# Flamingo block with a two-of-eight expert layer: the order of gathers, indexed stores and weight parts on GpSimd, and products of ones on TensorE

## The reference

```
logits = xf @ Wr + br
topk_val, topk_idx = top_k(logits, 2);  scores = softmax(topk_val)
h = xf @ W1[e] + b1[e];  a, g = split(h);  out_e = (silu(a) * g) @ W2[e] + b2[e]
out = sum over the two chosen e of scores * out_e
```

## Time and profile before

| what | value |
|---|---|
| median of 3 runs | 936.27 us (932.23, 936.27, 938.24) |
| the profiled execution's own time | 931.24 us |
| its span, first to last instruction | 929.4 us |
| mean granted TensorE clock | 0.985 of full speed |
| TensorE busy / VectorE / ScalarE / GpSimd | 95% / 60% / 56% / 40% |
| DMA queues of SyncE and of GpSimd, share of 16 engines | 21.3% and 3.4% |

### The profile page before, as it was taken

The page is one execution under the profiler, slowest core; times in us unless marked ns, Lnnn a source line. Parts: engine busy times, 40 slices in busy tenths (PEclk is TensorE's granted clock), DMA queues, the critical chain, the costliest instruction groups (busy, mean ns, idle before and its releaser), DMA issues.

```text
span 929.4 us, 20316 instructions
## 1 busy us (share of the span) xinstructions
PE 880.3 (95%) x6813; PEld 799.1 (86%) x6814; DVE 560.4 (60%) x1331; ACT 519.2 (56%) x1466; POOL 367.2 (40%) x530
## 2 busy tenths in 40 slices
PE   6989999999999979999999976999999999999996
PEld 4579999998898759999999976899999999987653
DVE  4666556556655763444434347877777876666456
ACT  6676777677776244344343452756655655652565
POOL 3173444444443224445454541434434443443000
PEclk9999999999999889999999998999999999999998
DMA  9000000420002457777776713000000000000002
GB/s 264 4 1 2 1 1 1 148 69 1 0 1 72 144 204 249 250 242 261 244 262 236 267 42 94 24 23 13 13 23 11 12 1 1 1 2 0 1 0 91
DMA packets 36674, 76.19 MB, mean 82 GB/s; under 512 B 4941, under 2 KB 22721, under 8 KB 36481
## 3 DMA queue, kind: packets, MB, share of 16 engines
q1 hardware_dynamic: 32865, 65.11, 21.3%
q0 software_dynamic: 3744, 10.23, 3.4%
HBM read 66.02 MB, written 9.31 MB: 81 GB/s over the span
## 4 chain that ended last, share of the span: by engine, by line
PE 85%; DVE 6%; DMA 3%; issue 2%; ACT 2%; POOL 1%; SPq 0%; DVEq 0%; POOLq 0%; ACTq 0%
PE banks L535 16%; PE banks L537 15%; PE banks L536 15%; PE banks L1530 14%; PE banks L573 8%; PE banks L563 5%; PE banks L427 2%; PE banks L1809 2%; PE banks L1820 1%; PE banks L1814 1%; PE banks L1802 1%; PE banks L1520 1%; PE banks L542 1%; DMA y_rows<-region_b,home_now 1%; DVE region_b L1404 1%
## 5 line engine op out<-in xcount | busy, mean ns | idle before, releaser
L1084 ACT ACTIVATE region_a<-banks,negmax 128x154 f32<-128x154 f32 (+1 forms) x384 | 161.7, 434 | 29.1 <-DVE negmax L877 28.0
L1530 PE MATMUL banks<-region_b,region_a 128*128 128x128 f32 x1248 | 148.4, 278 | 1.2 <-ACT region_b L1565 1.2
L1530 PEld LDWEIGHTS banks<-region_b,region_a 128*128 128x128 f32 x1248 | 145.4, 195 | 1.8 <-ACT region_b L1565 0.9
L1230 POOL TENSOR_TENSOR region_a<-region_a,recip 128x640 f32<-128x640 f32 x64 | 80.3, 1255 | 137.4 <-DVE recip L881 137.4
L1193 POOL TENSOR_TENSOR region_a<-region_a,recip 128x512 f32<-128x512 f32 x64 | 66.7, 1042 | 138.6 <-DVE recip L881 99.5
L877 DVE TENSOR_REDUCE negmax<-banks 128x4 f32<-128x616 f32 (+1 forms) x128 | 100.4, 785 | 28.3 <-PE banks L563 15.5
L1620 DVE SCALAR_TENSOR_TENSOR region_b<-banks,region_a,region_b 128x128 f32<-128x128 f32 x156 | 43.9, 344 | 104.3 <-PE banks L1530 104.3
L573 PE MATMUL banks<-ident,region_a 128*128 128x128 f32 x640 | 94.5, 279 | 3.9 <-DVE pT_low L887 1.6
L573 PEld LDWEIGHTS banks<-ident,region_a 128*128 128x128 f32 x640 | 72.7, 141 | 14.2 <-issue 9.8
L535 PE MATMUL banks<-xT_high,Wq_high 128*128 128x256 f32 x256 | 77.8, 304 | 3.8 <-DVE q_low L863 2.0
L1066 ACT CAST pT_high<-banks 128x640 fp32r<-128x640 f32 x64 | 44.4, 694 | 65.1 <-PE banks L573 65.1
(11 more groups left out here) (294 smaller groups left out, 2495.0 us busy)
## 6 DMA issues: line engine op xcount, KB each, us to landing
region_a<-in_L_ffn_W SPq DMA_DIRECT2D x39, 1024.0 KB, 5.4
W<-in_L_ffn_W SPq DMA_DIRECT2D x1, 4096.0 KB, 15.9
W<-y_rows SPq DMA_DIRECT2D x16, 256.0 KB, 2.8
out<-x SPq DMA_DIRECT2D x8, 256.0 KB, 2.2
x<-in_x SPq DMA_DIRECT2D x1, 1536.0 KB, 13.7
region_b<-in_L_xattn_Wq SPq DMA_DIRECT2D x1, 1024.0 KB, 9.4
region_b<-in_L_xattn_Wo SPq DMA_DIRECT2D x1, 1024.0 KB, 14.6
xn_rows<-region_b SPq DMA_DIRECT2D x1, 1024.0 KB, 4.8
```

Of the source, the lines that this page charges most:

```text
L1084: e = act.activation(into, source, ACT.Exp, bias=negmax[:, n % 2, u:u + 1], accum_out=sums[:, n % 2, u:u + 1])
L1230: pool.tensor_tensor(probs1[:, n % 2], probs1[:, n % 2], rc, ALU.mult).then_inc(sem("p_norm"), 1)
L1530: mm = pe.matmul(banks[:, 2 * r + part, m * P:(m + 1) * P], W1[r][:, k, cols], xgT[:, r, k, :], start=(k == 0), stop=(k == DK - 1))
```

## The change

Three edits.

1. GpSimd: in turn j the gather is that of slot j + 4 in place of slot j + 3, still ahead of the store of slot j. The gather of slot 3 moves ahead of turn 0. With it go the waits: `xgt_ps` and `token_now_ready` for j + 2, and the copy of row numbers is that of slot j + 5.
2. GpSimd: the four query weight parts move behind the store of their turn.
3. TensorE: 16 products of ones ahead of the first slot's transpose, and 12 in place of 16 behind the wait for `gathered0`.

```diff
@@ pe_pairs
                 pe.wait_ge(sem("gathered0"), 16)
-                pe_warm(pe, 16)
+                pe_warm(pe, 12)
             pe.wait_ge(sem("xn_ready"), t0 + 2)
@@ pe_experts
             pe.wait_ge(sem("kv1_raw"), len(KV1_UNITS) - 2)
+            pe_warm(pe, 16)
             turn_x(0, 0)
@@ pool_experts
             home_next(0, 0)
+            pool.wait_ge(sem("token_now_ready"), 1)
+            pool.wait_ge(sem("xgt_ps"), 1)
+            pool.wait_ge(sem("xg_in1"), 16)
+            tokens_now(RING + 1, 1)
+            gather_x(0)
 
             def emit(i):
                 for j, r in body_tiles(i):
-                    if is_tile(j + 3):
-                        pool.wait_ge(sem("token_now_ready"), j + 1)
-                        pool.wait_ge(sem("xgt_ps"), j + 1)
                     if is_tile(j + 4):
-                        ahead, more = after(r, 1)
+                        pool.wait_ge(sem("token_now_ready"), j + 2)
+                        pool.wait_ge(sem("xgt_ps"), j + 2)
+                    if is_tile(j + 5):
+                        ahead, more = after(r, 2)
                         pool.wait_ge(sem(f"xg_in{ahead}"), 16 * (i + more + 1))
-                        tokens_now(j + 4, ahead)
-                    if is_tile(j + 3):
-                        gather_x(r)
-                    if query_part(j) is not None:
-                        n = query_part(j)
-                        pool.wait_ge(sem("query_high"), n + 1)
-                        pool.tensor_tensor(Wq_low_parts[:, n], Wq1_parts[:, n], Wq_high_parts[:, n].bitcast(F32),
-                                           ALU.subtract).then_inc(sem("query_low"), 1)
+                        tokens_now(j + 5, ahead)
+                    if is_tile(j + 4):
+                        gather_x(after(r, 1)[0])
                     pool.wait_ge(sem("home_now_ready"), j + 1)
                     pool.wait_ge(sem("ey_sb"), j + 1)
...
                     scatter_y(r)
+                    if query_part(j) is not None:
+                        n = query_part(j)
+                        pool.wait_ge(sem("query_high"), n + 1)
+                        pool.tensor_tensor(Wq_low_parts[:, n], Wq1_parts[:, n], Wq_high_parts[:, n].bitcast(F32),
+                                           ALU.subtract).then_inc(sem("query_low"), 1)
```

## The result

The changed kernel took 928.65 us in the median (926.03 to 932.60, 20 runs), the kernel before 935.59 us (931.35 to 940.14, 20 runs) beside it. The ratio is 0.9924, 95% interval 0.9909 to 0.9939: 6.9 us less. The forecast was 4.7 us less; the time lies in its range and in the case "within 1%". The two intervals do not overlap. In five measurements the median of the kernel before was 932.2 to 936.2 us, that of the changed kernel 928.7 and 929.5 us in two. All ratios here are of fast runs with fast runs, and they are not the quotients of the two medians.

A forecast was written before the change was run, and what follows sets the result against it. TensorE was taken as the bound (85% of the span), its steady 5.22 us turn unchangeable. Gains of 2.8 + 1.8 + 0.1 + 0 = 4.7 us from the 936.27 us median gave 931.5 us, range 925.5 to 937.

The forecast's parts named there:

- within 1%: Whole kernel: the change cannot be told from no change, since a measurement resolves about 1%; chance 0.83.
- Part 1: 16 products of ones fill TensorE's idle gap ahead of slot 0, so its hidden products run at full clock; 2.8 us.
- this just fits, by 0.3 us: Opening: VectorE, after `b2` lands at 345.2 us, finishes at 347.7 us; TensorE needs it for slot 0's output at 348.0.
- Rival A: Opening is bound by loads: `b2` or W1 comes 3 us later and the ones gain nothing; 934.4 us, chance 0.12.
- rival B: Slot 0's low clock is not in every launch, so ones ahead of it may gain nothing; about 934.4 us, chance 0.13.
- Part 2: Gathers issued one slot sooner on GpSimd remove TensorE's stall at slot 37's late transpose; 1.8 us.
- in other turns gathers are already in time: Expert stage outside slot 37: more lead for the gathers buys nothing.
- rival C: More gathers are late in ordinary runs than in the profiled one, so more is gained; 926.6 us, chance 0.15.
- Part 3: Query parts behind GpSimd's stores: slot 36's store goes out sooner, easing slot 37's; 0.1 us, between 0 and 1.3.
- Part 4: 12 ones behind `gathered0` start attention 1's transposes 0.4 to 0.6 us sooner, but VectorE's weight part hides it; 0.
- The end of the stage: Expert stage's last two stores keep their distance from TensorE's last products, being tied to VectorE's addition and the previous landing.
- Rival D: Two gathers under way beside a store make stores land later, 5.7 us per turn; 949.6 us, chance 0.04.

The follow-up runs named there:

- the slow launch: Kernel before with 24 products of ones ahead of slot 0, profiled on its slowest run, 939.46 us; measured 0.9976, median 934.74 against 936.20 us.

## Why the prediction was right, and where it was too small

The direction, the case and the range were right, and the mechanisms that the sum named are in the trace. Its sizes were off both ways, so it is in part luck that the sum of 4.7 us lies between the two measured gains, 6.9 and 3.3 us.

- **Part 1, predicted 2.8 us.** The step "at full clock slot 0's hidden products take what slot 1's take" held where at most 1.01 us were idle behind the ones: 3.84 us in three of three profiles (idle 0.61, 0.45, 1.01 us). It failed in two of two with 1.83 and 1.86 us idle: 5.47 and 5.41 us. The step "nothing is delayed, the gap hides all of it" took the gap of before, 3.75 us, as given: it is 3.5 to 4.1 us without the ones and 4.0 to 5.4 us with 16 of them. And "this just fits, by 0.3 us" failed. The landing of `b2`, put at 345.2 us, was sound; the step from it to the multiply was put at nothing and measures 1.26 to 1.31 us in the twelve profiles where `b2` stands behind W1 and its landing was recorded, the one of before among them. With it the prediction's own numbers give 349.0 us against the 348.0 that TensorE needs. The trace lost 0.5 us and not 1.0, since slot 1's products themselves came 0.46 us later than predicted (9.86 us behind the key and value products, not 9.40). The term was 2.35 - 0.49 = 1.9 us in the changed kernel's profile.

  Over all profiles, slot 2's hidden products start 17.2 to 17.6 us behind the key and value products without the ones, 15.5 to 15.8 us with 16 of them and a punctual gather (three profiles), 18.0 and 18.1 us with 16 and a late one (two), and 16.1 us with 24 (two). So 16 ones gain 1.8 us or lose 0.6, which fits that nothing clear was measured with them alone.

  Rival A was right in kind and small; rival B was wrong in this form: slot 0 was cold (6.0 to 6.7 us) in all seven profiles without the ones.
- **Part 2, predicted 1.8 us.** Slot 37's stall went, as forecast, and the stage from slot 2 to slot 38 is 1.57 us shorter. But the mis-sized step is "in other turns gathers are already in time". Slot 6's was not quite, even in the profile that the prediction read (0.69 us), and in other launches there are worse. Seven profiles with the old order of gathers have 1.8 to 2.5 us of turns over the pitch in five cases, 11.4 in one, and 4.5 where the query parts stood behind the store; seven with the new order have none over 0.11 us each from slot 2 on. This is rival C in kind, which I gave 0.15. Its size, 5 us on top of the 4.7, is not borne out: the runs with both GpSimd edits and with the gathers alone gave 2.3 us (0.1 to 4.6) and 1.7 us (-0.2 to 3.5). Late gathers may be why the gain was 6.9 us beside a slow measurement of before and 3.3 beside a fast one, but no run counts them in ordinary launches, so the cause of that difference is not shown.
- **Part 3, predicted 0.1 us.** By itself this edit costs 3.9 us; together with the lead it costs nothing that the runs can tell. The prediction's sentence "behind it stands the next gather, which has 11 us" named the cover, and the price without it is what the run with the old gathers shows. What I had not done is work out that price.
- **Part 4, predicted 0.** Right within what can be measured; 0.5 us by the profiles' average. The row of 5.34 us is one of a spread from 3.84 to 6.61 us for the same 16 products, and at its upper end they hold up the transposes by 1.3 us, which "VectorE hides it" left out.
- **The end of the stage** "keeps its distance" but for chance: the wait of the last store was 2.2 to 4.4 us over the profiles, with long ones in both orders. 1.3 of the 4.1 us between the two spans are of this kind.
- **Rival D** (stores land later) came in kind, without a price. GpSimd waits for landings of stores for 0 to 9.5 us in the seven profiles with the old order (3.9 on the average) and for 5.2 to 16.8 us with the new one (9.6). The slowest store of a profile lands in 4.55 to 5.32 us with the old order and in 5.45 to 6.00 us with the new one, where landings were recorded; the median stays at 3.0 to 3.2 us. No turn grew by more than 0.11 us.

## What to carry to other kernels

A prefetch that is in time in one profile can be late in others if it stands behind a wait for another transfer: compare its lead with the slowest landing, not with the median, and count what a missed start costs at the consumer's clock. Price each edit also without the edit that covers it, since moving work behind a store was worth nothing with the lead and -3.9 us without. Filler on TensorE pays only if it reaches up to the transfer that it bridges in every launch, and the transfer may itself come later with the filler in place; a little too much (0.5 us by slot 2) was cheaper here than a little too little (2.4 us). When a load "just fits", count also what the waiting engine still does between the landing and its first instruction.

## What the runs showed of the hardware that I had not expected

- TensorE's clock fell to half behind 1.83 to 2.40 us of idle time in a stretch that was busy on both sides (slot 0 with 16 ones, slot 37 with the query parts behind, the turn behind slot 4's products in the slow launch; five cases in all), and not behind 0.45 to 1.58 us (seven cases). A wait for data of 2 us cost about 4.
- Behind a transpose from slot 2 on that waited for data, the first output product waited 0.23 to 0.61 us more for issue, in all eight cases of the profiles. Slot 6's gather in the profile of before, landed 0.44 us ahead of its transpose, had such a wait of 0.42 us behind it too.
- The same indirect gather landed in 2.9 us in the median, while in each of the twelve profiles with recorded landings at least one gather of slots 36 to 38 took 5.4 to 6.6 us, whether it was issued 2.2 us or about 1 us ahead of a slot's products. Why is open.
- With the ones in the program a 16 KB instruction fetch came some 6 to 9 us sooner, within 1.4 us of the end of the key and value products and not 7.1 to 8.2 us behind it. The gather that was then on its way landed in 5.4 to 6.5 us, not 4.4 to 5.2; the link between the two is not shown.
